# A mixture-of-experts dispatch reordered: totals and ranks ahead of the turns, routing in three bursts, class state added by bf16 rows, squares ahead of the evictions

## The reference

```python
x = x + gated_shift(ln_c(x))        # tanh gates of a 3x3x3 convolution, rolls along the images
t = tokens(x)
t = t + moe0(ln_t(t))               # 8 experts 64 -> 256 -> 64, each token goes to its best 2
x = image(t)
x = x + conv3x3_of_signs(ln_c(x)) * factor
t = tokens(x)
t = t + moe1(ln_t(t))               # experts chosen per image, 64 -> 128 -> 64, layer norm at the end
x = image(t)

def moe0(xf):                       # the part that the change prepares
    top_w, top_i = top_k(xf @ Wg + bg, 2)
    top_w = softmax(top_w)
    out = sum over e of w_dense[:, e] * (gelu(xf @ W1[e] + b1[e]) @ W2[e] + b2[e])
```

## Time and profile before

| | us |
|---|---|
| median of three runs | 2552.9 (2551.2 to 2553.08) |
| the profiled execution, its own time | 2551.47 |
| its span in the trace | 2549.6 |
| mean clock granted to PE over the span | 0.838 of full |
| the dispatch phase, from the first `add` to the start of the last scatter | 295.2 to 953.67 |

### The profile page before, as it was taken

One profiled execution on the slowest core, in us unless ns is written; L12 is line 12 of the kernel. 1 busy time (PEld: TensorE's weight loads), 2 busy tenths in 40 slices (PEclk: granted clock), 3 DMA queues, 4 the chain that ended last, 5 costly groups with the idle time before them and its releaser, 6 DMA issues. The chain is left out here.

```text
span 2549.6 us, 32816 instructions
## 1 busy us (share of the span) xinstructions
PE 1811.4 (71%) x8144; PEld 1045.0 (41%) x8144; DVE 1460.1 (57%) x3427; ACT 1144.1 (45%) x2248; POOL 1100.1 (43%) x1400
## 2 busy tenths in 40 slices
PE   8986433332424318999999997488888883798887
PEld 4652221221212105555555553265565552343333
DVE  6651466666565625666666664276666664345445
ACT  5650111111111106777677774254544552566665
POOL 3330046766666673333333333777777740000000
PEclk9997655555555558999999998599999996899999
DMA  5457521221222001111111111133333322755551
GB/s 171 157 139 161 146 66 57 68 61 52 71 59 74 27 25 47 58 56 57 56 58 57 56 58 51 25 102 102 102 102 111 104 92 90 180 159 166 152 173 62
DMA packets 189502, 230.31 MB, mean 90 GB/s; under 512 B 56531, under 2 KB 170804, under 8 KB 189236
## 3 DMA queue, kind: packets, MB, share of 16 engines
q1 hardware_dynamic: 164276, 202.60, 27.0%
q0 software_dynamic: 25088, 26.14, 4.3%
HBM read 111.73 MB, written 116.88 MB: 90 GB/s over the span
## 5 line engine op out<-in xcount | busy, mean ns | idle before, releaser
L646 POOL DMA_INDIRECT scr_rows<-row,place_int x392 | 404.9, 1033 | 124.3 <-issue 124.3
L1243 POOL DMA_INDIRECT y_returned<-scr_y,place_of_token x392 | 377.1, 962 | 132.4 <-issue 116.8
L673 PE MATMUL token_psum<-centre_and_gate,x_now 128*128 128x144 f32 x392 | 102.2, 452 | 346.9 <-DVE x_now L802 346.9
L1025 POOL CAST w_now<-w1all 128x512 fp32r x252 | 155.0, 615 | 376.3 <-PE y_psum L1061 364.2
L1108 ACT ACTIVATE hidden<-hidden_psum,w_now 128x512 f32<-128x512 f32 x504 | 304.5, 691 | 1.2 <-PE hidden_psum L1050 1.2
L1050 PE MATMUL hidden_psum<-page_tokens,w_now 128*128 128x512 f32 x1008 | 268.9, 409 | 1.6 <-DVE page_tokens L1136 1.6
L1061 PE MATMUL y_psum<-hidden,w_now 128*64 128x512 f32 x1008 | 244.1, 605 | 0.0
L673 PEld LDWEIGHTS token_psum<-centre_and_gate,x_now 128*128 128x128 f32 x392 | 93.9, 331 | 365.9 <-issue 334.0
L1050 PEld LDWEIGHTS hidden_psum<-page_tokens,w_now 128*128 128x128 f32 x1008 | 180.4, 189 | 136.6 <-issue 100.6
L203 PE MATMUL ln_var<-ln_sq,average 128*128 128x448 f32 x448 | 210.2, 554 | 22.4 <-DVE ln_q L225 20.0
L225 DVE SCALAR_TENSOR_TENSOR ln_q<-ln_var,ln_rr 128x448 f32<-128x448 f32 x224 | 138.9, 620 | 151.9 <-ACT ln_rr L220 151.5
(11 more groups left out here) (204 smaller groups left out, 3417.7 us busy)
## 6 DMA issues: line engine op xcount, KB each, us to landing
tokens<-scr_split SPq DMA_DIRECT2D x112, 224.0 KB, 3.7
page_rows<-scr_rows SPq DMA_DIRECT2D x126, 132.0 KB, 2.1
scr_y<-y_rows SPq DMA_DIRECT2D x126, 128.0 KB, 1.7
scr_rows<-zero_rows SPq DMA_DIRECT2D x14, 924.0 KB, 4.3
scr_xn<-xn SPq DMA_DIRECT2D x56, 224.0 KB, 2.0
scr_split<-hi SPq DMA_DIRECT2D x56, 224.0 KB, 2.5
scr_split<-lo SPq DMA_DIRECT2D x56, 224.0 KB, 2.7
tokens_plus_y<-scr_xn SPq DMA_DIRECT2D x56, 224.0 KB, 2.7
```

The lines of the kernel that those rows point to most:

```text
L646: pool.indirect_dma_start(out=R, out_offset=bass.IndirectOffsetOnAxis(ap=idx[:, u, 2 * px + a:2 * px + a + 1], axis=0), in_=row[:, u, px, ...
L673: mm = pe.matmul(tps[:, b, q, (P + 2 * E) * s:(P + 2 * E) * (s + 1)], xa[:, b, PG * k:PG * k + PG], cenw[:], start=True, stop=True)
L1025: pool.tensor_copy(w1s[:, b, t].rearrange("p l h -> p (l h)"), w1all[:, bass.ds(e, 1)].rearrange("p o l h -> p (o l h)")).then_inc(w_done, 1)
L1243: pool.indirect_dma_start(out=y[:, h % 3, k // 2, k % 2, :], out_offset=None, in_=Y, in_offset=bass.IndirectOffsetOnAxis(ap=PLACE[:, at:at ...
```

## The change

- PE: `total` and `rank` half 0 stay at m = 1, but `turn` now stands at m = 0 (first pair) and m = 2 (second pair), and `rank` half 1 at m = 2 ahead of that turn. So at m = 1 no turn stands ahead of `total`.
- DVE: `add` runs twice at m = 0 and once at m = 1 and m = 2. `route` is cut in three: 0 to 31 at m = 0, 32 to 51 at m = 1, 52 to 57 at m = 2, the last behind an `add` and a `sums`.
- ACT: both `keep_x` of a pair run together, then `seeds`, then `evict`, which now squares first, then copies the logits, and last copies the rows (and waits for the scatters).
- The class state is split on DVE into a high and a low bf16 row, with two operations more in a round (46 and 47), and the third matmul of `rank` takes these two rows in bf16 in place of one in float32.
- `countdown`, `key`, `chosen`, `both` and `first` become bf16, and `both` is laid out expert by expert, so that the `is_class` products read rows that lie together.

```diff
@@ -510,13 +510,13 @@
...
 L = sbuf(ctx, "logits", [P, TG, E])
-countdown = sbuf(ctx, "countdown", [P, TG, E])
-key = sbuf(ctx, "key", [P, TG, E])
-chosen = sbuf(ctx, "chosen", [P, 2, TG, E])
+countdown = sbuf(ctx, "countdown", [P, TG, E], BF16)
+key = sbuf(ctx, "key", [P, TG, E], BF16)
+chosen = sbuf(ctx, "chosen", [P, 2, TG, E], BF16)
 rest = sbuf(ctx, "rest", [P, TG, E])
-both = sbuf(ctx, "both", [P, TG, E])
+both = sbuf(ctx, "both", [P, E, TG], BF16)
 best = sbuf(ctx, "best", [P, 2, TG])
-first = sbuf(ctx, "first", [P, 2, TG])
+first = sbuf(ctx, "first", [P, 2, TG], BF16)
 gap = sbuf(ctx, "gap", [P, TG])
...
@@ -531,13 +531,15 @@
...
 raw = sbuf(ctx, "before_raw", [P, P])
-one = sbuf(ctx, "one_row", [1, P])
+minus = sbuf(ctx, "minus_rows", [2, P], BF16)
 ones = sbuf(ctx, "ones_class", [P, NC])
...
 pairs = sbuf(ctx, "pairs", [P, 2, NC])
-NXT = sbuf(ctx, "next", [P, 2, NC])
-NL = sbuf(ctx, "next_less_limit", [P, 2, NC])
+NEXT = sbuf(ctx, "next_and_next_less_limit", [P, 2, 2, NC])
+NHI = sbuf(ctx, "next_high", [2, 2, NC], BF16)
+NPARTS = sbuf(ctx, "next_parts_negated", [2, 2, 2, NC], BF16)
+NXT, NL = NEXT[:, :, 0], NEXT[:, :, 1]
 LIM = sbuf(ctx, "limit", [P, NC])
...
@@ -568,7 +570,7 @@
...
 HT = HC * TG
-INV, TOP, SCAN, PLACE0, DONE = 5, 8, 32, 50, 56
+INV, TOP, SCAN, PLACE0, DONE = 5, 8, 32, 52, 58
 PREPARED = 4 + E + 9 + 1 + 1
...
@@ -685,25 +687,28 @@
...
             pe.wait_ge(routed, DONE * r + (PLACE0 if h else SCAN + 1))
-            for k, state in enumerate((NXT, NL)):
+            for k in range(2):
                 o = vps[:, k, 0:HT]
...
                 pe.matmul(o, every[:], run[:, classes, :].rearrange("p c g -> p (c g)"), start=False, stop=False)
-                mm = pe.matmul(o.rearrange("p (c g) -> p c g", g=TG), one[:],
-                               state[0:1, u, classes].unsqueeze(2).broadcast_to([1, HC, TG]),
+                mm = pe.matmul(o.rearrange("p (c g) -> p c g", g=TG), minus[:],
+                               NPARTS[:, u, k, classes].unsqueeze(2).broadcast_to([2, HC, TG]),
                                start=False, stop=True)
...
         def step(i, m):
-            if m % 2 == 1 and there(i, m - 1):
-                turn(i, m - 1)
+            if m % 4 == 0 and there(i, m):
+                turn(i, m)
             if m % 4 == 1 and there(i, m - 5):
...
                 rank(i, m - 5, 0)
-                rank(i, m - 5, 1)
-
-        every_step(pe, step, 2)
+            if m % 4 == 2 and there(i, m - 6):
+                rank(i, m - 6, 1)
+            if m % 4 == 2 and there(i, m):
+                turn(i, m)
+
+        every_step(pe, step, 3)
 
...
@@ -717,17 +722,6 @@
...
             act.wait_ge(turned, h + 1)
-            wait(act, scattered[b], 56 * (h - b))
-            dst = row[:, u, k0:k0 + HPX, :, 0:C]
-            for (lo, hi), n in zip(PARTS, (1, 2)):
-                src = blocks(b % 2, lo, hi, 0, P)
-                if hi == 6:
-                    o, src = dst[:, 0:6].rearrange("p (q k) a c -> p q k a c", k=3), src.rearrange("p q k (a c) -> p q k a c", a=2)
-                    for q in range(2):
-                        ins = act.activation(o[:, q], src[:, q], ACT.Copy)
-                else:
-                    ins = act.activation(dst[:, 6], src.rearrange("p (a c) -> p a c", a=2), ACT.Copy)
-                ins.then_inc(copied, 1)
             wait(act, summed, h - 1)
...
@@ -746,6 +740,17 @@
...
                 act.activation(o, src, ACT.Copy).then_inc(kept, 1)
+            wait(act, scattered[b], 56 * (h - b))
+            rows_now = row[:, u, k0:k0 + HPX, :, 0:C]
+            for (lo, hi), n in zip(PARTS, (1, 2)):
+                src = blocks(b % 2, lo, hi, 0, P)
+                if hi == 6:
+                    o, src = rows_now[:, 0:6].rearrange("p (q k) a c -> p q k a c", k=3), src.rearrange("p q k (a c) -> p q k a c", a=2)
+                    for q in range(2):
+                        ins = act.activation(o[:, q], src[:, q], ACT.Copy)
+                else:
+                    ins = act.activation(rows_now[:, 6], src.rearrange("p (a c) -> p a c", a=2), ACT.Copy)
+                ins.then_inc(copied, 1)
 
...
@@ -755,12 +760,13 @@
...
         def step(i, m):
-            if there(i, m):
+            if m % 2 == 0 and there(i, m):
                 keep_x(i, m)
-            if m % 2 == 1 and there(i, m - 1):
-                evict(i, m - 1)
+                keep_x(i, m + 1)
             if m % 4 == 0 and there(i, m - 4):
                 seeds(i, m - 4)
+            if m % 2 == 0 and there(i, m):
+                evict(i, m)
 
...
@@ -773,13 +779,13 @@
...
         dve.memset(every[:], 1.0).then_inc(prepared, 1)
-        dve.memset(one[:], 1.0).then_inc(prepared, 1)
+        dve.memset(minus[:], -1.0).then_inc(prepared, 1)
         dve.memset(ones[:], 1.0).then_inc(prepared, 1)
...
         dve.memset(G[:], 0.0).then_inc(prepared, 1)
-        dve.memset(NXT[:], 0.0).then_inc(prepared, 1)
-        dve.memset(NL[:], 0.0).then_inc(prepared, 1)
+        dve.memset(NEXT[:], 0.0).then_inc(prepared, 1)
+        dve.memset(NPARTS[:], 0.0).then_inc(prepared, 1)
         dve.wait_ge(consts, 16 * 6)
...
@@ -862,7 +868,7 @@
...
                 elif s == 19:
-                    ins = dve.tensor_tensor(both[:], chosen[:, 0], chosen[:, 1], ALU.add)
+                    ins = dve.tensor_tensor(both[:].rearrange("p e g -> p g e"), chosen[:, 0], chosen[:, 1], ALU.add)
                 elif s == 20:
...
@@ -876,8 +882,8 @@
...
                     ins = dve.tensor_tensor(isc[:, c0:c0 + k, :],
-                                            both[:, :, e + 1:E].rearrange("p g e -> p e g"),
-                                            both[:, :, e].unsqueeze(1).broadcast_to([P, k, TG]), ALU.mult)
+                                            both[:, e + 1:E, :],
+                                            both[:, e].unsqueeze(1).broadcast_to([P, k, TG]), ALU.mult)
                 elif s == 31:
...
@@ -918,25 +924,30 @@
...
                 elif s == 46:
+                    ins = dve.tensor_copy(NHI[:], NEXT[0:2, 1 - u])
+                elif s == 47:
+                    ins = dve.scalar_tensor_tensor(out=NPARTS[:, 1 - u], in0=NHI[:], scalar=page[0:2, 0:1],
+                                                   in1=NEXT[0:2, 1 - u], op0=ALU.mult, op1=ALU.subtract)
+                elif s == 48:
                     ins = dve.tensor_copy(G[:], end[:, NC - 1:NC])
-                elif s in (47, 50):
-                    h = int(s == 50)
+                elif s in (49, 52):
+                    h = int(s == 52)
                     dve.wait_ge(ranked, 2 * r + h + 1)
...
                         op0=ALU.is_ge, op1=ALU.mult)
-                elif s in (48, 51):
-                    h = int(s == 51)
+                elif s in (50, 53):
+                    h = int(s == 53)
                     half = places[:, HT * h:HT * h + HT]
                     ins = dve.tensor_tensor(half, vps[:, 0, 0:HT], half, ALU.add)
-                elif s in (49, 52):
-                    h = int(s == 52)
+                elif s in (51, 54):
+                    h = int(s == 54)
                     ins = dve.tensor_tensor(places[:, HT * h:HT * h + HT], places[:, HT * h:HT * h + HT],
                                             isc[:].rearrange("p c g -> p (c g)")[:, HT * h:HT * h + HT], ALU.mult)
-                elif s == 53:
+                elif s == 55:
                     ins = dve.tensor_reduce(pos[:], place[:].rearrange("p c g -> p g c"), AX.X, ALU.add)
-                elif s == 54:
+                elif s == 56:
                     ins = dve.tensor_copy(idx[:, u], pos[:])
...
@@ -944,17 +955,23 @@
...
         def step(i, m):
-            if there(i, m):
+            if m % 4 == 0 and there(i, m):
                 add(i, m)
-            if m % 4 == 2 and there(i, m - 2):
-                sums(i, m - 2)
-            if m % 4 == 0 and there(i, m - 2):
+                add(i, m + 1)
+            if m % 4 == 0 and there(i, m - 4):
                 sums(i, m - 2)
                 route(i, m - 4, 0, SCAN)
+            if m % 4 == 1 and there(i, m):
+                add(i, m + 1)
             if m % 4 == 1 and there(i, m - 5):
-                route(i, m - 5, SCAN, DONE)
-
-        every_step(dve, step, 2)
+                route(i, m - 5, SCAN, PLACE0)
+            if m % 4 == 2 and there(i, m):
+                add(i, m + 1)
+                sums(i, m - 2)
+            if m % 4 == 2 and there(i, m - 6):
+                route(i, m - 6, PLACE0, DONE)
+
+        every_step(dve, step, 3)
         dve.tensor_tensor(named[:], pairs[:], TAB[:].unsqueeze(1).broadcast_to([P, 2, NC]), ALU.mult)\
...
         dve.wait_ge(named_done, 1)
```

## The result

The changed kernel takes **2462.6 us** (median of 4 runs, 2457.08 to 2463.75) against 2552.05 for the one before, a ratio of 0.9648 with a 95% interval of 0.9630 to 0.9665: 3.5% faster. The forecast was 2475.5, in a range of 2459 to 2508. Way and mechanism were right, the gain was 13 us larger than forecast.

The account below looks back on a forecast made before the run. The loop releasing POOL bounds the dispatch, then POOL's own 38.2 us rounds: first round -6.9, POOL's 13 gaps -74.3, round starts +3.9, together -77.3 to 2474.2, plus 1.4 for the median: 2475.5 us, range 2459 to 2508.

Parts of the forecast that it names:

- The bound and its floor: Dispatch rounds: the loop releasing POOL binds at pitch 43.96 us; floor 5.7 below, POOL's own work 38.2 a round.
- all three waits: DVE's loop: waits of 71.0 us for ranks, 60.0 for squares and 48.8 for totals, 13.8 a round.
- DVE's loop: DVE's round after the change: 30.1 + 0.45 - 0.9 = 29.7 us, with remaining waits some 30.
- the wait for rank half 1: DVE's wait for PE's second rank half: 0 to 0.6 us stays, or 2.6 at the float32 price.
- -0.9 for the tiles: DVE's bf16 tiles, mainly the seven is_class products: -0.9 us a round, bounds -0.6 and -1.2.
- The first round: Ahead of the first scatter, not bound by POOL: DVE's gains count whole, -6.9 us, from 345.84 to 339.0.
- the 0.3 of a scatter's gap: POOL between rounds: each start without idle time still costs 0.3 us, +3.9 in all.
- Rival 1: Third burst on DVE holds up scatters as the scan does: 2.8 us a round, +39, 2514 us; chance 0.09.
- scatters over the third burst above 1 us: Sign in the changed profile that the forecast is wrong: scatters over DVE's third burst take over 1 us.
- Rival 2: POOL is held up less, saving 0.9 us in all rounds: -12, 2463 us; chance 0.08.
- Rival 3: Row buffers bind as scatter landings pile up, and it gets slower: 2572 us at a 24 us landing; chance 0.03.
- rival 4: An unseen wait of more than 8 us a round stays in DVE's loop: 2513 with half the gap; chance 0.04.

Follow-up runs that it names:

- half the scatters: Changed kernel with 14 of the 28 scatters of each round left out: 2357.1 us in a single run.
- the order alone: Changed kernel with the class state added from one float32 row and countdown, key, chosen, both and first in float32, old layout: 2466.1 us, ratio 0.9660.
- section 4: Three kernels, each with one change at DVE's scan in the changed kernel: second scan 2477.1 us, second sum 2471.0, scan's mask in PSUM 2451.6.
- the data alone: Kernel before with bf16 rows for the class state and the bf16 tiles, in the old order on all engines: 2514.8 us, ratio 0.9853.
- the eight sums: Changed kernel with eight more reductions a round on DVE, ahead of the scan: 2544.1 us, ratio 0.9969.
- the first kernel with the mask in PSUM: Changed kernel with the scan in two halves of 392 and its mask in PSUM in place of SBUF: 2451.6 us, ratio 0.9606.

## Why the prediction was right, and by how much it missed

**The bound and its floor** were right: POOL issues without a pause, pitch 37.8 where 38.5 was forecast. All of the 74.3 us of gaps are gone, and the earlier trace rows named all three waits that made them.

**DVE's loop**, 29.7 in the sum, was 30.9 with half the scatters. Single terms were off, and none mattered: the wait for rank half 1 stays for 2.6 us in all, -0.9 for the tiles was about -0.5 (the seven products fell by 1.0, from 2.71 to 1.73, and `both` took back 0.7 of it), as these rows of DVE in order of time show:

```profile
576.15 1.12 DVE L871 TENSOR_TENSOR both<-chosen 128x224 bf16<-128x224 bf16 x1
...
578.20 1.73 DVE L884 TENSOR_TENSOR is_class<-both 128x196 bf16<-128x196 bf16 x7
```

**The first round**, -6.9, measured -7.9 (345.84 to 337.98). The `add` behind the scan came at 324.13, 2.3 us earlier than the 326.44 of the earlier trace rows, where I had 1.3.

**The term that was mis-sized** is the one I gave least thought: "I give each the 0.3 of a scatter's gap, +3.9", on top of a round of 38.2. From the first start to the end of the last scatter I had 538.4 us, and it was 865.36 - 337.98 = 527.4. The 11.0 us split up so. Between rounds POOL lost 0.02 instead of 0.3: 3.6. And inside my 38.2 lay what the starts of rounds had cost, which I had taken for POOL's work in every round. Before the change a round took 0.66 to 0.80 us from L643 to its first scatter in all but two rounds; now it is 0.34 in all but the first: 4.6. This has two causes. In seven rounds L643 took its 0.18 and the scatter came 0.48 behind it instead of 0.16; so it did in 12 rounds with half the scatters, where POOL waited 7 to 11 us for each. That is a restart after waiting. In five rounds L643 itself took 0.64 or 0.65, because it started inside DVE's `add` L800, as in the first three rows here (POOL and DVE in order of time, kernel before). The last two rows are from the kernel with the order alone, whose L643 had not waited:

```profile
566.41 0.63 DVE L800 TENSOR_TENSOR x_now<-X,shifted 128x448 f32<-128x448 f32 x1 [0.21 <-DVE place_of_token L942]
566.44 0.65 POOL L643 TENSOR_TENSOR passed<-passed 1x1 f32<-1x1 f32 x1 [5.26 <-DVE place_of_token L942]
...
567.24 1.32 POOL L646 DMA_INDIRECT scr_rows<-row,place_int  x1 [0.16 <-issue]
```
```profile
417.03 0.62 DVE L806 TENSOR_TENSOR x_now<-x_now,own 128x448 f32<-128x448 f32 x1
417.23 0.47 POOL L643 TENSOR_TENSOR passed<-passed 1x1 f32<-1x1 f32 x1
```

In both L643 ends 0.05 behind DVE's operation. So POOL's small addition is held by the rule of section 4, idle or not.

And in four rounds before, the second scatter came late, as here (POOL in order of time, kernel before):

```profile
523.14 0.99 POOL L646 DMA_INDIRECT scr_rows<-row,place_int  x1 [0.48 <-issue]
525.69 1.17 POOL L646 DMA_INDIRECT scr_rows<-row,place_int  x1 [1.56 <-issue]
```

There are none of these in the changed kernel: 4.6. They stand in the 5th, 8th, 11th and 14th round, with the data alone and with the eight sums too, and in the 9th alone with half the scatters; in the 14th with the data alone POOL had not waited ahead. So waiting is not the whole of it, and the cause stays open. The delays of the scatters went the other way, from 25.8 to 27.5, 1.7. The idle time by issue in the scatters' group, 117.9 us now and 124.3 before, would have told me of the gaps.

**Rival 1** (the third burst holds up scatters) had a true mechanism at a price nine times too high. The reading of the earlier trace rows was wrong: the scatter of 601.22 was not spared because L935 is harmless, but because it had started 0.23 us ahead of it. Now, in 12 rounds, a scatter that starts inside the second L946 takes 1.33, 0.36 more. That is 4.3 us (4.6 with the 13th, which takes 1.25), not 39, since only the part that is left of a 0.57 us operation is paid. So one sign of being wrong that the prediction names, scatters over the third burst above 1 us, did appear, at a small price. **Rival 2**'s time, 2463, was met, but by the starts of the rounds and not by fewer delays. **Rival 3** is excluded by the landing of 1.9 us, and **rival 4** by the single wait of L645.

## What to carry to other kernels

When one engine issues a fixed row of transfers and waits for another in between, take its floor from a round without idle time, and look whether the start of a round costs more than the gap itself, by restarting or by what it starts beside. Two edits that shorten the same loop do not add up once another engine binds: measure the slack (leave half of the binding work out, or add idle work to the other engine), then drop what brings nothing. A single instruction beside another proves nothing on contention; sort all of them by where they start.

## What the runs showed of the hardware

An indirect transfer issued by POOL is held by a DVE operation with two SBUF inputs only if it starts inside it. It then takes the rest of that operation plus 0.77 or 0.78 us (scans, 130 cases), 0.84 to 0.86 (most of the others; up to 1.03 in an `add`) or 0.37 (the bf16 `both` with its strided output, all 74 scatters that it delayed), and never less than the 0.96 to 0.97 undisturbed. One SBUF input, or one and a PSUM input, holds nothing (140 cases in the sums, 21 in the scan of the first kernel with the mask in PSUM). A small addition on POOL is held in the same way and ends 0.05 us behind DVE's operation.

With the mask in PSUM a scan of 392 elements takes 0.97 us, two halves 1.98 against 1.79 for the whole from SBUF. A bf16 addition of 224 elements that writes with a stride takes 1.12 us against 0.39 in float32 without one. After waiting, POOL takes 0.48 instead of 0.16 us from its small addition to the next transfer, in 12 of 13 waits with half the scatters. The second transfer of a round came 0.5 to 1.3 us late in four rounds of three kernels; what that is, no run here settles.
